# Mixer of a two-stage transformer block: token and gate-row transfers cut into pieces of 128 KB, one per attention step, and the cast of the scan's result moved from VectorE to ScalarE

## The reference

```python
mod = (_silu(L0_c) @ L0_wmod).reshape(L0_c.shape[0], 6, 1, -1)
sa, ca, ga, sb, cb, gb = (mod[:, 0], mod[:, 1], mod[:, 2], mod[:, 3], mod[:, 4], mod[:, 5])
...                                       # ga and gb are kept at least 0.25 away from zero
h = _layernorm(x) * (1 + ca) + sa
x = x + ga * block(h)                     # attention, scan, gates, dense MLP
h = _layernorm(x) * (1 + cb) + sb
x = x + gb * experts(h)                   # top 2 of 8 experts, gated MLP each
```

```python
xn = _layernorm(x, ln1_g, ln1_b)
attn = _windowed_attn(xn, W_qkv, W_O, b_O)       # each window of 64 sees itself and the one before
ug = xn @ W_ug + b_ug
u, g = ug[..., :128], jax.nn.sigmoid(ug[..., 128:])
drive = xn @ B_w + u
s_t = A * s_(t-1) + drive_t                      # the scan, along the 512 tokens
x = x + g * attn + (1.0 - g) * (states @ C_w)
h = _layernorm(x, ln2_g, ln2_b)
x = x + gelu(h @ mlp_W1 + mlp_b1) @ mlp_W2 + mlp_b2
```

## Time and profile before

| | us |
|---|---|
| median of 3 runs | 2137.33 (2129.54 to 2142.75) |
| profiled execution, its own time | 2147.33 |
| its span | 2145.6 |
| first store of the mixer's tokens | 108.87 |
| last store of the mixer's tokens | 939.07 |
| busy in the span: PE, DVE, ACT, POOL | 1805.8, 1474.6, 965.5, 1072.1 |
| granted TensorE clock, mean | 0.917 |

### The profile page before, as it was taken

How to read it: one execution, slowest core, us unless ns; L and a number is a source line. 1 busy time by engine, 2 the same in 40 slices (tenths; PEclk the granted TensorE clock), 3 DMA queues, 4 the chain that set the end, 5 groups by cost and what they waited for, 6 DMA issues and landing times. The chain is left out here.

```text
span 2145.6 us, 65560 instructions
## 1 busy us (share of the span) xinstructions
PE 1805.8 (84%) x23596; PEld 1405.0 (65%) x23597; DVE 1474.6 (69%) x3321; ACT 965.5 (45%) x1734; POOL 1072.1 (50%) x1262
## 2 busy tenths in 40 slices
PE   4788888888888888969988898870899999999997
PEld 2566666666666665746665566550788888888886
DVE  6777776677776766767888888872456666666665
ACT  3233333333333333436545454530566555666664
POOL 5223333333333332325677776773466666666665
PEclk7899999999999999989988988885899999999999
DMA  4222221221211222124334433430455545454553
GB/s 145 62 56 57 56 57 56 56 57 56 56 42 49 56 54 60 48 74 127 116 114 127 142 110 118 127 89 28 91 95 90 91 92 94 88 91 90 94 92 55
DMA packets 155644, 174.93 MB, mean 82 GB/s; under 512 B 35140, under 2 KB 136199, under 8 KB 155328
## 3 DMA queue, kind: packets, MB, share of 16 engines
q1 hardware_dynamic: 101248, 96.90, 16.3%
q0 software_dynamic: 36352, 56.78, 14.2%
q10 hardware_dynamic: 17856, 18.37, 2.5%
HBM read 109.40 MB, written 53.99 MB: 76 GB/s over the span
## 5 line engine op out<-in xcount | busy, mean ns | idle before, releaser
L1911 POOL DMA_INDIRECT out<-experts_y,experts_entry x144 | 237.2, 1647 | 190.7 <-DVE experts_y L1887 163.6
L816 ACT ACTIVATE mixer_prob<-mixer_sc 128x1024 f32<-128x1024 f32 x128 | 131.1, 1025 | 315.3 <-PE mixer_sc L670 315.3
L1852 DVE TENSOR_SCALAR experts_v<-experts_v 128x512 f32<-128x512 f32 x144 | 73.4, 510 | 220.3 <-ACT experts_v L1826 215.4
L670 PE MATMUL mixer_sc<-mixer_Qh,w_Kz 64*128 64x128 f16 x2048 | 137.9, 224 | 92.2 <-issue 92.2
L1035 POOL TENSOR_TENSOR mixer_oTl<-mixer_on,mixer_oTh 128x128 f16<-128x128 f32 x128 | 55.5, 434 | 308.6 <-ACT mixer_oTh L823 307.9
L1826 ACT ACTIVATE experts_g<-experts_pg,x_b 128x256 f32<-128x256 f32 x288 | 121.0, 471 | 180.5 <-PE experts_pv L131 179.3
L1901 POOL DMA_INDIRECT experts_rows<-scratch_xs,experts_entry x144 | 170.4, 1184 | 59.2 <-issue 43.3
L922 DVE TENSOR_REDUCE w_mx<-mixer_sc 128x8 bf16<-128x1024 f32 x128 | 156.4, 1222 | 37.6 <-PE mixer_sc L644 37.6
L670 PEld LDWEIGHTS mixer_sc<-mixer_Qh,w_Kz 64*128 64x128 f16 x2048 | 104.1, 98 | 111.5 <-issue 97.9
L1526 POOL DMA_INDIRECT scratch_queue<-mlp_entry,mlp_slot x128 | 141.1, 1102 | 52.4 <-issue 38.6
L129 PE MATMUL experts_pg<-experts_xT,x_w 128*128 128x256 f16 x576 | 158.1, 275 | 10.4 <-issue 7.3
(11 more groups left out here) (372 smaller groups left out, 5816.8 us busy)
## 6 DMA issues: line engine op xcount, KB each, us to landing
mixer_x<-in_x SPq DMA_DIRECT2D x16, 512.0 KB, 10.7
w_Kz<-mixer_Kt SPq DMA_DIRECT2D x64, 128.0 KB, 2.7
mixer_hres<-mixer_h SPq DMA_DIRECT2D x16, 512.0 KB, 4.7
scratch_xs<-scratch_mod SPq DMA_DIRECT2D x16, 512.0 KB, 10.6
scratch_x<-mixer_x SPq DMA_DIRECT2D x16, 512.0 KB, 2.9
mlp_xa<-scratch_x SPq DMA_DIRECT2D x16, 512.0 KB, 4.3
mlp_stage<-in_x_w SPq DMA_DIRECT2D x16, 512.0 KB, 4.3
mlp_xb<-scratch_x SPq DMA_DIRECT2D x16, 512.0 KB
```

The source lines that it names most:

```text
L670: last = pe.matmul(sc[:, 2 + h, at:at + P], Kz[half_rows(h), j, i, c, keys], queries(q, h, c, n), start=False, stop=(c + j == 2 and i == 1))
L816: act.activation(prob[:, n % 2, :].rearrange("p (c j) -> p c j", c=2), sc[:, 2:4, :], ACT.Exp, scale=SCALE).then_inc(exped.sem, 1)
L1852: dve.tensor_scalar(v[:, q, :], v[:, q, :], -8.0, 10.0, ALU.max, ALU.min).then_inc(v_cut.sem, 1)
L1911: pool.indirect_dma_start(out=out, out_offset=bass.IndirectOffsetOnAxis(ap=entry[:, s, t, 0:1].bitcast(I32), axis=0), in_=y[:, s % 2, t, : ...
```

## The change

The gate rows are written in four transfers of 128 rows, and the tokens are loaded in four of 128 tokens. The first gate piece waits as before (in the samples that load; in the last two for nothing of h but the maximum of step 0), each other piece for the maximum of the next step: gate 0, gate 1, tokens 0, gate 2, tokens 1, gate 3, tokens 2, tokens 3 behind the maxima of steps 0 (or h) to 7. The modulation is loaded behind the last piece. The counters of these transfers count four pieces in place of one. The cast of `st` to `sth` leaves VectorE's step 0 and stands in ScalarE's step 1, between the exponential and the gates.

```diff
+            def load_tile(b, t):
+                sp.dma_start(x[:, t, :], din["x"][bass.ds(b, 1), t * P:(t + 1) * P, :].rearrange(
+                    "a p d -> (a p) d")).then_inc(x_in.sem, 16)
+
             def load_x(b):
-                sp.dma_start(x[:], din["x"][bass.ds(b, 1), :, :].rearrange("a (t p) d -> p (a t) d", p=P)
-                             ).then_inc(x_in.sem, 16)
+                for t in range(TT):
+                    load_tile(b, t)
...
+                gate = scratch["mod"][bass.ds(b, 1), 5 * D:6 * D].to_broadcast([P, D])
+                for n, (part, t) in enumerate((("gate", 0), ("gate", 1), ("x", 0), ("gate", 2), ("x", 1), ("gate", 3),
+                                               ("x", 2), ("x", 3))):
+                    if more and n == 0:
+                        sp.wait_ge(s_h.sem, s_h.at(b, 4))
+                    else:
+                        sp.wait_ge(maxed.sem, maxed.at(b, n + 1))
+                    if part == "gate":
+                        sp.dma_start(scratch["xs"][bass.ds(b * L + t * P, P), D:2 * D], gate
+                                     ).then_inc(gate_out.sem, 16)
+                    elif more:
+                        load_tile(b + 2, t)
                 if more:
-                    sp.wait_ge(s_h.sem, s_h.at(b, 4))
-                gate = scratch["mod"][bass.ds(b, 1), 5 * D:6 * D].to_broadcast([L, D])
-                sp.dma_start(scratch["xs"][bass.ds(b * L, L), D:2 * D], gate).then_inc(gate_out.sem, 16)
-                if more:
-                    load(b + 2)
+                    load_modulation(b + 2)
                 sp.wait_ge(x1_sb.sem, x1_sb.at(b, TT))
...
+                    if s == 1:
+                        act.wait_ge(scanned.sem, scanned.at(b, 1))
+                        act.copy(sth[:], st[:]).then_inc(st_hi.sem, 1)
                     if s < 2:
                         open_gates(b, s)
...
                         dve.tensor_tensor_scan(st[:], w["A"][:, 0:1].to_broadcast([P, L]), drv[:], 0.0, ALU.mult,
                                                ALU.add).then_inc(scanned.sem, 1)
-                        dve.wait_ge(scanned.sem, scanned.at(b, 1))
-                        dve.tensor_copy(sth[:], st[:]).then_inc(st_hi.sem, 1)
```

More of the change, by code:

```diff
@@ L444, in mixer @@
         out_bank = [pm[:], sc[:, 2, :], sc[:, 3, :], pv[:]]
-        x_in = m.counter("x_in", 32)
+        x_in = m.counter("x_in", 16 * TT + 16)
         dve_passed, pool_passed = m.counter("dve_passed"), m.counter("pool_passed")
@@ L491, in mixer @@
         x1_out = m.counter("x1_out", 16)
-        gate_out = m.counter("gate_out", 16)
+        gate_out = m.counter("gate_out", 16 * TT)
         h_first = m.counter("h_first")
@@ L568, in _ @@
             sp.wait_ge(start.v_in.sem, 16 * 7)
-            sp.wait_ge(gate_out.sem, 16 * NB)
+            sp.wait_ge(gate_out.sem, 16 * TT * NB)
         @block.tensor
@@ L860, in layer_norms @@
             if part == 0:
-                dve.wait_ge(x_in.sem, x_in.at(b, 32))
+                dve.wait_ge(x_in.sem, x_in.at(b, 16 * TT + 16))
                 moments(dve, b, x, range(TT))
@@ L975, in _ @@
             start.silu(dve)
-            dve.wait_ge(x_in.sem, 16)
+            dve.wait_ge(x_in.sem, 16 * TT)
             moments(dve, 0, x, range(TT))
@@ L986, in _ @@
             dve.wait_ge(s_norm0.sem, 4)
-            dve.wait_ge(x_in.sem, 32)
+            dve.wait_ge(x_in.sem, 16 * TT + 16)
             for n, (i, op) in enumerate(((1, ALU.mult), (0, ALU.add))):
```

## The result

The changed kernel takes 2012.2 us (median of 4 runs, 2009.69 to 2015.08) against 2137.94: 0.9416 of the time before, 95% interval 0.9384 to 0.9449. I had said 2021 within 1998 to 2075. The profiled execution takes 2012.55, 134.8 less than the one of before.

A forecast was written before the change was run, and what follows sets the result against it. TensorE's instruction fetch, late behind SP's queued transfers, was taken to stall each ordinary sample. Savings 100.5 + 2.6 + 13.6 = 116.7 took the profiled 2147.33 to 2030.6; for the median 2021, range 1998 to 2075.

The forecast's parts named there:

- The stall and its cause: Ahead of the score products, samples 1 to 13: TensorE's instruction fetch, late behind SP's queued transfers, stalls it 7.09 each.
- 1.0 for meetings of pieces and fetches: Per sample, loss remaining where pieces coincide around a fetch: 1.0 of the 8.73, ends 0 and 3.5.
- How long a piece holds the engines: In the burst of 1280 KB, each 128 KB was taken to hold the DMA engines for 1.2.
- the 1.25 in hand: At TensorE's fetch: 8.1 late cost only 6.85, so TensorE has 1.25 in hand before it stalls.
- the 2.4 I feared: First two gate pieces, back to back around the fetch of step 2: 2.4 of holding, less 1.25, up to 1.15 lost.
- my own rule: For a fetch meeting a piece: TensorE loses the time the piece holds the engines, less the 1.25 in hand.
- The 3.6 for the last token piece with the modulation: Last token piece and modulation, issued together: 384 KB hold the engines 3.6, up to 2.35 lost if a fetch falls there.
- The first sample: Sample 0 has its own stall of 5.28; half was taken as saved, 2.6, ends 0 and 5.3.
- The cast: Moved to ScalarE, it removes TensorE's 0.97 of idleness ahead of step 1's transpose: 14 x 0.97 = 13.6, ends 0 and 33.5.
- B: Rival: queued bytes aren't the cause, the fetch stays as late, only the cast counts; 2124, chance 0.06.
- C: Rival: a fetch waits for a transfer's whole latency and all six per sample meet one; slower, 2256, chance 0.06.
- The sum: Over the whole kernel: 100.5 for samples 1 to 13, 2.6 for sample 0, 13.6 for the cast, 116.7 in all.

The follow-up runs named there:

- Gate pieces twice: The changed kernel with every gate piece written a second time, into the left half of the same rows; 2095.98 us, ratio 0.9803.
- pieces at once: The changed kernel with the same eight pieces issued one right behind the other when the modulated h is ready, modulation last; 2064.89 us, ratio 0.9679.
- before, gate rows early: The kernel before with one line moved: gate rows whole at the start of the sample, cast still on VectorE; 2020.79 us, ratio 0.9494.

## Why the prediction was right, and where it was off

**The stall and its cause: right.** Seven microseconds per sample were a late instruction fetch behind SP's transfers. Sample 14 of before was the control, and the experiments agree with it: a fetch costs TensorE more than 0.2 per sample only where it is due while gate rows are queued. The loss went wholly: with the clock back at 1.00, a sample with loads costs 47.41 - 47.19 = 0.22 more than one without, where I had left 1.0 for meetings of pieces and fetches.

**How long a piece holds the engines: wrong in size, and right by luck.** I spread the burst evenly, 1.2 per 128 KB. Gate rows take about 1.9 (512 KB at 70 GB/s is 7.5), tokens and modulation about 0.4 (768 KB in 2.5). My reason for cutting to 128 KB was that 1.2 is under the 1.25 in hand; 1.9 isn't, and two gate pieces back to back are 3.8, more than the 2.4 I feared. By my own rule a fetch that meets a whole one loses about 0.6. It came out well by where the fetches fall. In sample 4 they come 0.7, 5.8, 10.2 and 14.6 behind the first gate issue. The first packet of a transfer moves about 1.4 behind its issue, so the fetch of step 2 passes ahead of the first two pieces, and the next comes when they are nearly through. Little is lost with the cast on VectorE either (0.9493 with pieces only, its fetch of step 2 at 2.3 to 3.5). "Gate pieces twice" shows the other side. The key transfers were a weak witness for small pieces: of the two instruction packets in their stretch, the first stands 0.4 behind the first issue, before a packet of theirs moves. The 3.6 for the last token piece with the modulation is really 1.2, within what is in hand.

**The first sample: undersized.** 7.2 and not 2.6. Its stall of 5.28 is gone whole, with the slow clock behind it (0.73 from 96 to 108.87 before, 1.00 from 84 to 101.67 after). It is the pieces: with them alone the first store stands at 101.46, with the cast alone at 108.07.

**The cast: 13.6 said, 14 to 17 measured.** Sample 14 gained 0.86 by the whole change, but its gate rows changed too: it takes 48.05 before, 46.98 with the cast only and 48.30 with pieces only, so the cast gives 1.07 to 1.11 there and the pieces take back some 0.2. Over samples 1 to 13 pieces with and without it differ by 1.18; 14 samples of 1.07 to 1.18 are 15 to 17. The ratios are 0.9493 without it and 0.9416 and 0.9428 with it, intervals apart; the differences are 14 and 16 us. The step in which it stands gained a little more than TensorE's 0.97 of idleness: from exponential to exponential it took 4.50 (296.56 less the row below, of the kernel before) and takes 3.34.

```profile
292.06 1.02 ACT L816 ACTIVATE mixer_prob<-mixer_sc 128x1024 f32<-128x1024 f32 x1 [1.06 <-PE mixer_sc L670]
```

What I had wrong is that the cast on its own leaves the stall as it is (2124 under B): it moved it by one fetch and cut it by a third, 2103.56. I read the stall as a length and not as an order of two events, one of which the cast moves. POOL's second product didn't get shorter either, 3.15 as before: the cast wasn't what stretched it.

**B, the unchanged stall, and the round robin.** The Trainium skill, DMA: Bandwidth & Descriptors, "Queues, rings and completion order", would let a fetch pass after one packet of the other queue, whatever else is queued (a packet of the page is a group of descriptors). The runs disagree with this: with the cast only, the caught fetch was served 9.8 to 12.6 behind the first issue, when 61 to 100% of the burst's bytes had started. With pieces at once it was served when 33 to 66% had, behind three pieces or more. Behind tokens and modulation alone it was served 1.7 late, when 98% or more of the 768 KB had started ("before, gate rows early"). It looks as if a fetch waits for what was queued ahead of it, but that is inferred from times alone; what makes it wait stays open.

**C, the loss by number of transfers,** is refuted by the changed kernel itself, with nine transfers and no stall. Doubled gate pieces, though, give back two thirds of the gain: 2095.98.

**The sum.** 100.5 + 2.6 + 13.6 = 116.7 said for the profiled execution; 121.8 + 7.2 + 0.9 = 129.9 measured in the mixer, and 4.9 outside that is spread between executions. Of the 18.1 by which the profiled time beats my 2030.6, 8.7 are in samples 1 to 13 (121.8 against 100.5 and 13 x 0.97), 4.6 in sample 0, and 4.9 that spread; sample 14 is 0.1 short.

## What to carry to other kernels

When TensorE idles with no releaser at the same place of each pass of a loop, look at the instruction packets in the DMA view around it: a fetch can be late behind the kernel's own transfers. Find the slow transfer first, by GB/s in short windows, before cutting all of them; here one line moved to where nothing is fetched (0.9494) did as much as eight pieces with the cast left alone (0.9493). Look at the first pass by itself: there the moved line still met a fetch. And treat such a stall as a race between two events: an edit that moves either one changes it.

## What the runs showed of the hardware

- Copying one 1 KB row of HBM to 512 rows of HBM moved at about 70 GB/s and landed in 9.6; the same rows stored from SBUF landed in 4.1. The DMA share while it moved was anything from 0.16 to 0.94, so that share alone doesn't show whether a fetch will wait.
- Instructions, TensorE's by the order of packets and stalls, came in packets of 16 KB (163 packets, 2.67 MB over the span, in both kernels), nine per loop pass. The Trainium skill, Runtime: NRT & Kernel Launch, "Instruction fetch mechanics", gives blocks of that size and calls the cost mostly hidden. The size agrees. The cost was hidden in sample 14 of before; in sample 4, where the fetch was 8.1 late, 6.85 of it showed, and 7.09 on the mean of 13 samples.
- VectorE's cast of 128x512 took 2.39 beside POOL's product and 0.43 in sample 15, where POOL had none; on ScalarE it took 0.61 in every sample. The tile's rows before and after (ns, shortest, median and longest):

```profile
L948 DVE CAST mixer_sth<-mixer_st x16: 428/2397/2401, 61.0 to 907.3; 128x512 f16<-128x512 f32 x16
```

```profile
L832 ACT CAST mixer_sth<-mixer_st x16: 610/610/611, 66.1 to 780.0; 128x512 f16<-128x512 f32 x16
```
